# Two modulators as two rows of one matmul, spread over the partitions by DMA, in a fused four-layer kernel

## The reference, cut to what matters

```
ctx   = causal_ema(x, tau_ctx)                      # scan over time
wg    = sigmoid([x, ctx] @ Wg.T + bg)
gated = x * wg
h1    = gelu(x @ Wn1.T + bn1)                       # (b, t, 128)
mod   = 0.5 + sigmoid(h1 @ Wn2.T + bn2)             # (b, t, 2): two modulators per time step
traces[d]   = causal_ema(gated * mod[..., d], tau_d)   for d = 0, 1
temporal    = sum_d traces[d] * softmax(blend)[d]
gate  = sigmoid(temporal @ Wtemp.T + btemp)
soma  = gelu(x @ Wsoma.T + bsoma)
out   = layernorm((soma * gate) @ Wout.T) * gamma + beta
x     = x + out
```

## Time and profile before

| what | value |
|---|---|
| median of 3 runs | 737.13 us (737.09 to 737.3) |
| span of the profiled execution | 734.0 us |
| time around the span (median less span) | 3.1 us |
| PE busy | 672.6 us, 92% |
| DVE busy | 541.1 us, 74% |
| ACT busy | 353.3 us, 48% |
| POOL busy | 177.6 us, 24% |
| one group in the steady state | 69.62 us |

### The profile page before, as it was taken

The page is one execution under the profiler, slowest core; times in us unless marked ns, Lnnn a source line. Parts: engine busy times, 40 slices in busy tenths (PEclk is TensorE's granted clock), DMA queues, the critical chain, the costliest instruction groups (busy, mean ns, idle before and its releaser), DMA issues.

```text
span 734.0 us, 7942 instructions
## 1 busy us (share of the span) xinstructions
PE 672.6 (92%) x2808; PEld 493.9 (67%) x2808; DVE 541.1 (74%) x737; ACT 353.3 (48%) x710; POOL 177.6 (24%) x220
## 2 busy tenths in 40 slices
PE   4969979265899999999999999999999999999996
PEld 1545444134677877778687868786877787787884
DVE  2665888766898688759766976697668758875965
ACT  1143376445356625653474357344724563465235
POOL 5002456656152300420132022102310220031001
PEclk9989999767899999999999999999999999999999
DMA  7896799679930970295039305820880040004001
GB/s 212 292 367 185 162 236 306 197 136 339 327 66 0 167 121 0 67 188 90 1 95 191 58 1 127 169 49 22 150 160 14 0 115 2 0 10 106 0 2 57
DMA packets 52470, 87.87 MB, mean 120 GB/s; under 512 B 8256, under 2 KB 10304, under 8 KB 52430
## 3 DMA queue, kind: packets, MB, share of 16 engines
q0 software_dynamic: 16896, 33.56, 27.7%
q1 hardware_dynamic: 32046, 53.79, 20.8%
q10 hardware_dynamic: 3488, 0.01, 0.3%
HBM read 64.27 MB, written 23.09 MB: 119 GB/s over the span
## 4 chain that ended last, share of the span: by engine, by line
PE 80%; DMA 6%; DVE 5%; POOL 3%; ACT 3%; issue 1%; SPq 1%; POOLq 0%; ACTq 0%; DVEq 0%
PE bank L1055 21%; PE bank L1057 20%; PE bank L1056 20%; PE bank L1095 3%; PE bank L1111 3%; PE bank L956 3%; PE bank L1158 2%; PE bank L1120 2%; DMA xr<-beside_scratch 2%; DMA beside_scratch<-xb 2%; PE bank L1085 2%; PE bank L1051 2%; DMA local_scratch<-xts 2%; DMA xts<-in_xT 1%; POOL xts L546 1%
## 5 line engine op out<-in xcount | busy, mean ns | idle before, releaser
L1556 DVE TENSOR_TENSOR_SCAN tr<-alpha,carry,tr 128x512 f32<-128x512 f32 x48 | 58.9, 1268 | 0.0
L593 POOL TENSOR_TENSOR rs_a<-ss_a,consts 128x1 f32<-128x1 f32 x32 | 10.5, 329 | 197.8 <-ACT hb L744 196.9
L1550 DVE SCALAR_TENSOR_TENSOR tr<-wgb,blend_w,mod 128x512 f32<-128x512 f32 x64 | 46.0, 750 | 10.7 <-ACT mod L769 9.9
L1055 PE MATMUL bank<-xh,wg_l 128*128 128x512 f32 x128 | 52.9, 413 | 0.0
L1055 PE MATMUL bank<-th,wg_l 128*128 128x512 f32 x128 | 52.0, 406 | 0.0
L1056 PE MATMUL bank<-xl,wg_h 128*128 128x512 f32 x128 | 50.4, 394 | 0.0
L1057 PE MATMUL bank<-xh,wg_h 128*128 128x512 f32 x128 | 50.3, 393 | 0.0
L1057 PE MATMUL bank<-th,wg_h 128*128 128x512 f32 x128 | 50.1, 391 | 0.0
L1056 PE MATMUL bank<-tl,wg_h 128*128 128x512 f32 x128 | 49.9, 390 | 0.0
L546 POOL TENSOR_TENSOR xts<-xb 128x2040 f32<-128x2040 f32 x8 | 29.3, 3662 | 65.0 <-DVE xb L1445 52.8
L1051 PE MATMUL bank<-xb,probT 128*128 128x512 f32 x64 | 39.3, 700 | 4.4 <-DVE xb L1445 4.4
(11 more groups left out here) (247 smaller groups left out, 1984.9 us busy)
## 6 DMA issues: line engine op xcount, KB each, us to landing
x2b<-beside_scratch POOLq DMA_DIRECT2D x12, 1024.0 KB, 9.1
xr<-rows_scratch POOLq DMA_DIRECT2D x10, 1024.0 KB, 10.3
xb<-in_x SPq DMA_DIRECT2D x8, 1024.0 KB, 14.4
beside_scratch<-xb SPq DMA_DIRECT2D x8, 1024.0 KB, 9.5
result<-xr SPq DMA_DIRECT2D x7, 1024.0 KB, 4.4
local_scratch<-xts SPq DMA_DIRECT2D x6, 1024.0 KB, 11.2
x2b<-local_scratch SPq DMA_DIRECT2D x6, 1024.0 KB, 5.6
x2b<-rows_scratch POOLq DMA_DIRECT2D x6, 1024.0 KB, 15.1
```

What stands on the lines that cost most here:

```text
L1055: pe.matmul(acc, wl, xh_, start=start, stop=False)
L1550: ve.scalar_tensor_tensor(t[:, d], w, blend_w[:, d, k:k + 1], mod[:, d], ALU.mult, ALU.mult).then_inc(tr_in, 1)
L1556: ve.tensor_tensor_scan(t[:, d], alpha[:, 1 + d:2 + d].broadcast_to([P, GN]), t[:, d], 0.0 if first else carry[:, k, 1 + d:2 + d], ALU.mul ...
```

## The change

The two matmuls by replicated weights become one matmul by `wn2_col` (128 x 2), whose result is two rows on partitions 0 and 1. ScalarE's tanh and half-and-add run once over these two rows, in place in `nar`. SP then issues two DMAs, each of which reads one row of 2 KB 128 times and writes it to 128 partitions of `mod[:, d]` (256 KB). VectorE waits for both DMAs (`mod_in`) before it multiplies. The matmul moves ahead of PRE[0], and ScalarE's two steps move ahead of `keep_ctx` and the gate's tanh. `wn2_rep` and its two copies go.

```diff
@@ SP
+                    def spread_mod(g):
+                        sp.wait_ge(mod_half, g + 1)
+                        if g:
+                            sp.wait_ge(tr_in, 2 * KE * g)
+                        for d in range(2):
+                            sp.dma_start(mod[:, d],
+                                         mod_rows[d:d + 1].rearrange("o (r n) -> o r n", r=1).broadcast_to([1, P, GN]))\
+                              .then_inc(mod_in, 16)
+
                     for g in range(GROUPS - 1):
+                        spread_mod(g)
                         if g + 3 < GROUPS:
                             load_x2(g + 3)
...
+                    spread_mod(LAST)
@@ ACT
                     def mod_sigmoid(g):
-                        for d in range(2):
-                            n = 2 * g + d + 1
-                            act.wait_ge(mod_mm, n)
-                            act.activation(mod[:, d], bank[MOD[d]][:], ACT.Tanh, bias=bias_n2[:, d:d + 1], scale=0.5)\
-                               .then_inc(mod_sig, 1)
-                            act.wait_ge(mod_sig, n)
-                            act.activation(mod[:, d], mod[:, d], ACT.Identity, bias=ONE, scale=0.5)\
-                               .then_inc(mod_half, 1)
+                        act.wait_ge(mod_mm, g + 1)
+                        act.activation(mod_rows, bank[MOD][0:2], ACT.Tanh, bias=bias_n2[:], scale=0.5)\
+                           .then_inc(mod_sig, 1)
+                        act.wait_ge(mod_sig, g + 1)
+                        act.activation(mod_rows, mod_rows, ACT.Identity, bias=ONE[0:2], scale=0.5)\
+                           .then_inc(mod_half, 1)
...
                         n1_gelu(g)
+                        mod_sigmoid(g)
                         keep_ctx(g, 0)
                         sigmoid_gate(g, 0)
-                        mod_sigmoid(g)
@@ PE, in front(g), behind CTX[k]
                             if k == 0:
+                                pe.wait_ge(n1_act, g + 1)
+                                if g == 0:
+                                    pe.wait_ge(params_in, N_PARAMS)
+                                if g > 0:
+                                    pe.wait_ge(o_done, GT * (g - 1) + 3)
+                                pe.matmul(bank[MOD][0:2], wn2_col[:], nar[:], start=True, stop=True)\
+                                  .then_inc(mod_mm, 1)
...
                             by_x3(g, bank[PRE[k]][:], wg_h, wg_l, 0, chunk(k)).then_inc(pre_mm, 1)
-                            if k == 0:
-                                pe.wait_ge(n1_act, g + 1)
-                                if g == 0:
-                                    pe.wait_ge(wn2_set, 2)
-                                if g > 0:
-                                    pe.wait_ge(o_done, GT * (g - 1) + 3)
-                                for d in range(2):
-                                    pe.matmul(bank[MOD[d]][:], wn2_rep[:, d], nar[:], start=True, stop=True)\
-                                      .then_inc(mod_mm, 1)
@@ DVE
                             if k == 0:
-                                ve.wait_ge(mod_half, 2 * g + d + 1)
+                                ve.wait_ge(mod_in, 16 * 2 * (g + 1))
...
-                    for d in range(2):
-                        ve.tensor_copy(wn2_rep[:, d], wn2_col[:, d:d + 1].broadcast_to([P, P])).then_inc(wn2_set, 1)
```

More of the change, by code:

```diff
@@ L59, in build_program @@
         bias_n1 = sb("bias_n1", [P, 1])
-        bias_n2 = sb("bias_n2", [P, 2])
+        bias_n2 = sb("bias_n2", [2, 1])
         db_cols = sb("db_cols", [P, B])
@@ L140, in build_program @@
             hb1 = sb2("hb1", [P, GN])
-            wn2_rep = sb2("wn2_rep", [P, 2, P])
         z = nar
+        mod_rows = nar[0:2]
         x3f = soma
@@ L183, in build_program @@
         mod_half = sem("mod_half")
+        mod_in = sem("mod_in")
         pre_mm = sem("pre_mm")
@@ L217, in build_program @@
         rows2_set = sem("rows2_set")
-        N1, PRE, CTX, MOD = 1, (5, 0, 2, 5), (6, 1, 3, 6), (7, 4)
+        N1, PRE, CTX, MOD = 1, (5, 0, 2, 5), (6, 1, 3, 6), 7
         SOMA, OUT = (2, 3, 4, 7), (3, 4, 7, 0)
@@ L304, in build_program @@
             w_in = [sem(f"w_in{i}") for i in range(3)]
-            wn2_set = sem("wn2_set")
             w_hi = sem("w_hi")
@@ L645, in _ @@
                         load(wn2_col[:], wn2.rearrange("d p -> p d"))
-                        load(bias_n2[:], row(bn2, P))
+                        load(bias_n2[:], bn2.rearrange("(d o) -> d o", o=1))
                         for d in range(2):
@@ L1078, in x2_transposes @@
                             if g >= 0 and k == 0:
-                                pe.wait_ge(mod_sig, 2 * g + 2)
+                                pe.wait_ge(mod_sig, g + 1)
                             if g >= 0 and k == 2:
@@ L1144, in front @@
                             if k == 0:
+                                pe.wait_ge(n1_act, g + 1)
[5 more added lines that the diff above has]
+                                  .then_inc(mod_mm, 1)
+                            if k == 0:
                                 pe.wait_ge(x3T_hi, KE * g + 2)
```

## The result

The changed kernel takes 900.01 us (median of 4 runs, 897.93 to 903.89). The kernel before took 737.11 us on the same chip. The ratio is 1.2227, 95% interval 1.2187 to 1.2267: 22% slower. The forecast was 895, with 760 to 940 as its range. By the medians the growth is 162.9 us.

What follows compares the result with a forecast made beforehand. PE was taken to bound the kernel from group 1 on. Growth of 110.4 (groups 1 to 6), 27.6 (group 0) and 20.3 (last), 158.3 us on a 734.0 span plus 3.1 around it, gave 895.4; range 760 to 940.

Steps and rivals of the forecast that it cites:

- The door of SBUF: In the spread, all 256 reads go to partitions 0 and 1 through one door, at one engine's 24.6 GB/s.
- T: Time for moving the two spreads' 512 KB itself, without the fixed 1.3 us; taken as 21.3 us.
- Both landings over 15 us: Sign in the profile after: the two 256 KB spread DMAs each take over 15 us to landing.
- VectorE late by 18.8 us: Groups 1 to 6: scans 18.8 us late, less 2.9 reserve, plus 2.5 for half clock: 18.4 us a group.
- One matmul saves 0.86 us: On PE, one modulator matmul instead of two saves 0.86 us per group, 6.9 us at most.
- The earlier place: The modulator matmul, moved ahead of PRE[0], meets no wait on PE in groups 1 to 7.
- The copies that go: Group 0: dropping the `wn2_rep` copies removes PE's 10.2 us wait for them, but this is worth nothing.
- ScalarE's half of the work: ScalarE's four instructions become two, 1.39 us less, each as long as before; rows ready at 257.7 in group 1.
- Group 0 grows by 27.6 us: Spreads queue behind SP's loads: scans 29.4 us late, less 4.3 reserve, plus 2.5 for the clock.
- rival 1: The spread is hidden behind other work, deciding from T = 4.5 down: 730 to 745 us, chance 17%.
- Rival 2: The spread costs half the price, T = 10.7: 811 us, within 760 to 845; chance 16%.
- Rival 3: Spread takes longer still, as accumulating DMAs into `x2b` share the door: T over 27, over 940 us; chance 5%.

Runs made afterwards that it cites:

- e3: Changed kernel with the two spreads replaced by plain copies of all 128 partitions of `nar`, same bytes, wrong modulators: 760.93 us, ratio 1.0344.
- e7: Changed kernel with the two rows first written to DRAM (4 KB) and spread over the partitions from there: 771.41 us, ratio 1.0474.
- e9: Changed kernel with rows on partitions 0 and 64, the second row's spread issued from ScalarE's queue: 851.38 us, ratio 1.1533.
- e8: Changed kernel with the second row's spread issued from ScalarE's queue, rows still on partitions 0 and 1: 899.78 us, ratio 1.2189.
- e4: Changed kernel without any spread, `mod` set to ones once at the start, modulators left out of the result: 733.21 us, ratio 0.9994.
- e10: Changed kernel with modulators on 64 partitions each, copies bringing the other halves, GpSimd's accumulating transfers after them from group 1: 743.05 us, ratio 1.012.

## Why the prediction was right, step by step

- **The door of SBUF: right, its price right by some luck.** I chose 24.6 GB/s, one engine's pace, and T = 21.3 us, so 22.6 us from issue to data. The data were due at 280.5 in the coordinates of before, and VectorE started at 314.06 - 32.3 = 281.8, some 1.3 us later. e3, e7 and e9 against e8 show that it is the source's place. But no run ties its pace to that of one engine: 16 engines read there together, and the spread alone moved at 27 GB/s. Alone it took 21.2 and 22.0 us from issue to first product, less than forecast; beside the accumulating transfers, of which the sum had nothing, 24.0 to 24.7, more than forecast. One of my grounds was a misreading: the row of `xr<-rows_scratch` is an accumulating transfer (line 585 of the code before), so its 10.3 us said little of a plain spread from DRAM. In e7 such spreads of 256 KB landed in 3.0 to 4.4 us. The Trainium skill's figure ("SBUF — State Buffer", DMA port swizzle), 27 GB/s a port, is what the spread alone ran at, and its table, by which partitions 0 and 64 lie on two ports, fits e9. By its 19.3 us I would have come to 879, too low, since the accumulating transfers add some 3 us in groups 1 to 5: VectorE is 20.3 to 21.0 late there, and 17.5 and 18.3 in the last two.
- **Both landings over 15 us: right only in company.** In the last groups, where the spread is alone, the first transfer landed in some 12 us (the 11.9 of the landings above; 16.7 is the median of the last group's two). In group 1 the median of the two is 22.8.
- **VectorE late by 18.8 us, reserve 2.9, clock 2.5: growth 18.4 a group.** It was 19.3 on average (115.8 / 6) and 19.84 in group 1. PE stood for 16.79 us where 16.8 were said, by luck: VectorE was 1.3 us later than forecast, but the transposes between the pauses ran at half clock and took up 0.9 of it (1.97 us for 8 where 8 at full clock took 1.04), and the matmul saved 0.3 less. The missing part is in the busy time: +3.05 instead of 2.5 - 0.86 = +1.64. I had priced the half clock behind one pause, and it holds for both pieces of work in 312 to 332. And one matmul saves 0.54.
- **One matmul saves 0.86 us: wrong for two columns.** The records show why. Their matmuls last 592 ns with 2 as with 128 columns, the load of the weights 82 ns instead of 188, and yet the pair takes 0.95 us in the chain against 0.86. The matmuls beside it are further apart too. From the start of the matmul ahead of it to that of the second behind it, it is 1.61 us in e4 (325.02 to 326.63) and 1.32 in e10 (335.67 to 336.99), which is nearly all of the 0.32 between their groups. In e4 the next load of weights starts 0.86 us after that of the 2 columns ended, in e10 0.24 us after that of the 128, both put down to issue; why, no run here tells.
- **The earlier place meets no wait in groups 1 to 7: right.** PE's only wait at L1159 is in group 0.
- **The copies that go are worth nothing: right.** PE waited 12.2 us for `nar` where it had waited 10.2 for them.
- **ScalarE's half of the work: right.** 0.68 and 0.72 us for 2 partitions, as for 128. The rows were due at 257.7 + 32.3 = 290.0, and were there at 290.00.
- **Group 0 grows by 27.6 us: 28.6, by two errors that nearly cancel.** The whole shift is 32.3, of which 3.7 are there before `nar`. The first product came at 220.20 where 219.5 was said, but counted from `nar` it came 3.0 us sooner than forecast. The spread was issued at 195.95 and took 24.25 us to its first use, as in groups 1 to 5. From the landing of the adapter's second load, about 204.3, only 15.9 us passed, so the spread moved in part beside the loads and not only behind them. The trace scans start at 221.53, 26.3 us late from `nar`, and not 29.4. The second error is the reserve of 4.3 us, read from VectorE's sum alone. The matmul at 208.24 stood on a second chain with next to no reserve:

```profile
201.61 1.90 ACT L827 ACTIVATE wo_h<-wo_l_f 128x2048 fp32r<-128x2048 f32 x1
```

```profile
203.60 4.58 POOL L580 TENSOR_TENSOR wo_l<-wo_l_f,wo_h 128x2048 fp32r<-128x2048 f32 x1 [17.13 <-ACT wo_h L827]
```

These are of before: 203.60 + 4.58 = 208.18, and PE starts 0.06 us later, without a wait that a list would show. ScalarE's cast stands in its order behind the keeping of the traces (L784) and is late with the scans. After, the same two and PE:

```profile
231.03 1.89 ACT L836 ACTIVATE wo_h<-wo_l_f 128x2048 fp32r<-128x2048 f32 x1
```

```profile
233.01 4.49 POOL L591 TENSOR_TENSOR wo_l<-wo_l_f,wo_h 128x2048 fp32r<-128x2048 f32 x1 [42.91 <-ACT wo_h L836]
```

```profile
237.55 0.80 PE L1064 MATMUL bank<-xh,ws_l 128*128 128x512 f32 x1 [9.83 <-POOL wo_l L591]
```

ScalarE's cast is 29.4 us later than before, and so is GpSimd's; PE is 237.55 - 208.24 = 29.3 later. Less the 3.7 these are 25.7 and 25.6, against scans that are 26.3 late: the reserve was 0.7 us and not 4.3. Up to group 1's product another 3.0 come, where 2.5 were said for the clock.
- **Last group 20.3: right,** with 19.9.
- **The rivals.** A hidden spread (rival 1) would have needed T under 4.5; of the spreads only e7's, from DRAM, has that, and the write to DRAM ahead of it took the gain away. Rival 2, two rows at half the price, did not come even with two places and two queues. Rival 3's accumulating transfers do share, but cost 3 us and not 6 or more.

158.3 us were forecast; 162.9 came by the medians, and 168.0 in the profiled execution. Its parts are 115.8 where 110.4 were forecast, 28.6 where it was 27.6, 19.9 where it was 20.3, and 3.7 in the first part, for which nothing was forecast and which the change doesn't touch.

## What to carry to other kernels

Price a transfer by the place that it reads, not by its bytes alone: a row of one SBUF partition that was read 128 times moved at 27 GB/s in all, with all 16 engines at it, while the same row in DRAM or a second matmul with replicated weights (0.54 to 0.86 us of PE here) gives the same spread for far less. A reserve that is read from one chain is only an upper bound; look for every other thing that the waiting instruction needs, above all those that ended just before it started and so show as no wait. And before making a wait go away, ask what comes 2 us behind it.

## What the runs showed of the hardware

- One SBUF place read by all 16 engines gave 27 GB/s (the last spread, 825 to 844), or 24.7 to 26.5 by the time of 256 KB more (10.6 and 9.9 us). The DRAM row gave 512 KB in 4.1 us from issue to use.
- In e9's last group two transfers issued together on two queues were served almost one after the other: 144 packets against 37 in the first 11.2 us.
- Copies of 128 to 256 KB that land in 2.2 or 2.3 us alone took 6.6 and 7.6 us (medians) beside accumulating transfers of GpSimd, nearly whatever their size; a 4 KB write took about 5.
- An fp32 product with 2 columns of weights took 0.95 us in the chain, one with 128 columns 0.86, and the group distance differed by 0.32 (69.08 against 68.76).
